# Moving preparation units and masked bundles inside the fourteen-bundle round of a sixteen-head cross attention

## The chip, the core and the metric

The kernel runs on one core of a Trainium2 chip. It is one launch that carries out twelve layers one after the other; the metric is the device time of the whole launch in microseconds. Three runs of the kernel before took 3176.26, 3175.15 and 3161.47 us, median 3175.15 us.

The engines that matter here are TensorE (PE, with its weight loads shown apart as PEld), VectorE (DVE), ScalarE (ACT), GpSimd (POOL) and SyncE (SP), which issues the transfers. Each works through its own list of instructions in order and waits for the others on semaphores.

## The reference, cut to what matters

The seventh layer is the only one that the change touches. Batch 32, 64 queries per batch, 1601 keys, width 128, 16 heads of 8 dimensions; the mask is the same for all batches and heads.

```python
def _L2_xattn_ref(query, key, value, mask, W_q, W_k, W_v, W_o):   # NUM_HEADS 16, D_K 8
    Q = _split(query @ W_q.T)        # query: (32, 64, 128), the normalised x
    K = _split(key @ W_k.T)          # key and value: ctx_1024, (32, 1601, 128)
    V = _split(value @ W_v.T)
    scores = jnp.einsum('bhqd,bhkd->bhqk', Q, K) / jnp.sqrt(jnp.float32(D_K))
    scores = jnp.where(mask, -jnp.inf, scores)
    attn_w = jax.nn.softmax(scores, axis=-1)
    attn_w = jnp.nan_to_num(attn_w, nan=0.0)
    out = jnp.einsum('bhqk,bhkd->bhqd', attn_w, V)
    merged = out.transpose(0, 2, 1, 3).reshape(B, Sq, D_MODEL)
    return merged @ W_o.T
...
x = x + _L2_xattn_ref(_layernorm(x, axis=-1), ctx_1024, ctx_1024, mask_1x1xSxS2_bk1, ...)
```

## The kernel before

The layer is the function `many_head_cross_attention`. It is written as four separate lists, one for each of PE, DVE, ACT and POOL, and all of them walk the same loop variable `b`, the **bundle**. A batch has 14 bundles (`ROUND = 14`): seven steps of 256 keys (the last has 65 keys, one chunk), each for two halves of the heads. I call `b % 14` the **place** in the round, 0 to 13. Thirty-two batches give 448 bundles.

In bundle `b` TensorE does, in this order:

1. `less_max` (L2908; L2911 at the short places 12 and 13): it starts two PSUM banks `st` with minus the maximum of each row. The two instructions (gi 0 and 1) each wait on `exped`: the second may start only when ScalarE has finished the first of the two exponentials of bundle `b - 1`, since `st` has three banks.
2. at the three places in `ON_TENSOR` only, `less_out` (L2921): four matmuls that add the mask to the scores before the exponential.
3. `query_by_keys` (L2895): scores for bundle `b + 18` into `mx`, for the row maxima; these are 512 keys wide, except at places 8 and 9, where they are 65 keys wide. It waits on `topped`, that is until VectorE has read the banks.
4. `keys_by_query` (L2882): the scores of bundle `b` on top of `st`.
5. `values` (L2942): the products of bundle `b - 3` with the values, accumulated in `pv`; at place 3 there are none, and place 4 has two of them and a clearing matmul (L2936). At places 1 and 2 they are for the short step and half as many.
6. `prepare`: at most one preparation unit. All of them use the one bank `prep`, and each waits on `prep_read` until the unit before it has been read out.

A unit is `K` (L2963) or `V` (L2959), a quarter of the projected keys or values of a batch to come, read by ScalarE, `M` (L2967), the maxima turned, read by ScalarE, or one of the three closing units of a batch: `E1` (L2971) turns the result `pvs`; VectorE then computes `own` from it in `own_values` (L3056, L3057, L3058, L3061, four instructions linked by waits); `E2` (L2973) multiplies `own` and cannot start before `own_values` is done; VectorE copies that to `yT` (L3088); `E3` (L2976) applies the output weights, and VectorE adds the result to `x` (L3093). Quarter 3 of K and of V is 65 keys wide and short.

In bundle `b` VectorE does, in this order: `masked_max` (L3031, with L3030) for bundle `b + 18`, two instructions of 512 columns or four of 65; at place 9 the eight small operations of `negated_parts` (L3041 to L3050); unless the place is in `ON_TENSOR`, the mask by a minimum with `capT` after the exponential (L3077, two instructions, each after its exponential); at place 2 the copy of `pv` to `pvs` (L3082); and last what belongs to the E unit of this bundle, for which it waits on `prep_done`. ScalarE does the two exponentials (L3112, L3115) and the read-outs of K, V and M (L3125, L3128, L3131).

Where each unit stands is set by two small tables in the code, `PREPARED` (K and V, counted from place 10 of a round) and the tuple in `late` (M, E1, E2, E3, as a bundle number relative to the batch). Nothing is planned at run time.

Of the kernel before, what the change touches and what calls it, by code (L numbers as in the profile page):

```python
# [2721 lines left out]
def many_head_cross_attention(c, name):  # L2722
# [5 lines left out]
    HELD = 7  # L2728
    FIRST, LAST = -LEAD - ROUND, ROUND * (B - 1) + ROUND + 10
    BUNDLES = ROUND * B  # L2730
    PREPARED = {0: ("K", 0), 2: ("V", 0), 3: ("K", 1), 4: ("V", 1), 5: ("K", 2), 6: ("V", 2), 7: ("K", 3), 9: ("V", 3)}
    ON_TENSOR = (4, 7, 9)
    chunk = [min(P, KEYS - P * j) for j in range(KC)]
    part = [min(4, KC - 4 * m) for m in range(4)]
    with Stage(c, name) as s:
# [27 lines left out]
        V = Steps(s.sem("vector_steps"), (1, ["set"] + LN_V + [f"q{i}" for i in range(4)]))  # L2763
# [11 lines left out]
        def early(b):  # L2775

            n, i = divmod(b - FIRST, ROUND)
            if not 0 <= n < B or i not in PREPARED:
                return None
            kind, m = PREPARED[i]  # L2780
            return kind, n, m

        def late(b):

            for kind, at in (("M", -3), ("E1", 18), ("E2", 20), ("E3", 22)):
                n, off = divmod(b - at, ROUND)
                if off == 0 and 0 <= n < B:
                    return kind, n, 0
            return None

        prep_at = {}
        for b in range(FIRST, LAST):
            for unit in (early(b), late(b)):
                if unit:
                    prep_at[unit] = len(prep_at) + 1
# [6 lines left out]

        masked_here = lambda b: b % ROUND in ON_TENSOR

# [54 lines left out]
        def _(pe):  # L2859
# [119 lines left out]
            for b in range(FIRST, LAST):  # L2979
                now, then = of_bundle(b), of_bundle(b + LEAD)  # L2980
                if now:
                    if b % ROUND == 0:
                        pe.wait_ge(prep_read, prep_at["M", now[0], 0])
                    less_max(b, *now)
                    if masked_here(b):
                        less_out(b, *now[1:])
                if then:
                    n = then[0]
                    if (b + LEAD) % ROUND == 0:
                        pe.wait_ge(qb_made, n + 1)  # L2990
                        pe.wait_ge(prep_read, prep_at["K", n, 3])
                    query_by_keys(b + LEAD, *then)
                if now:
                    keys_by_query(b, *now, 0)
                    keys_by_query(b, *now, 1)
                for x in values_at(b):
                    values(x)
                prepare(early(b))
                prepare(late(b))

        @block.vector
        def _(dve):
# [61 lines left out]
            for b in range(FIRST, LAST):  # L3064
                then = of_bundle(b + LEAD)
                if then:
                    masked_max(b + LEAD, *then)
                    if (b + LEAD) % ROUND == ROUND - 1:
                        negated_parts(then[0])
                now = of_bundle(b)  # L3070
                if now and not masked_here(b):
                    step = now[1]
                    for gi in (0, 1):
                        k, j = (P, (2 * step, 2 * step + 2)) if step < 6 else (KREST, (KC - 1, KC))
                        x = pT[b % HELD][0:k, 0:j[1] - j[0], gi, :].rearrange("p c (h q) -> p c h q", q=S)
                        dve.wait_ge(exped, 2 * b + gi + 1)
                        nc.vector.tensor_tensor(x, x, capT[0:k, j[0]:j[1], :].unsqueeze(2).broadcast_to([k, j[1] - j[0], 4, S]), ALU.min)\  # L3077
                            .then_inc(capped, 1)
                n, off = divmod(b - ROUND - 2, ROUND)
                if off == 0 and 0 <= n < B:  # L3080
                    dve.wait_ge(pv_done, ROUND * (n + 1))
                    nc.vector.tensor_copy(pvs[:, :, :], pv[:, 0:256].rearrange("p (e q) -> p e q", e=2)).then_inc(pv_copied, 1)  # L3082
                unit = late(b)
                if unit and unit[0] == "E1":
                    own_values(unit[1])
                elif unit and unit[0] == "E2":
                    dve.wait_ge(prep_done, prep_at[unit])
                    nc.vector.tensor_copy(yT[:, :], prep[:, 0:S]).then_inc(prep_read, 1)  # L3088
                elif unit and unit[0] == "E3":
                    n = unit[1]  # L3090
                    r = slice(S * (n % 2), S * (n % 2) + S)
                    dve.wait_ge(prep_done, prep_at[unit])
                    nc.vector.tensor_tensor(c.x[r, n // 2, :], prep[r, 0:D], c.x[r, n // 2, :], ALU.add).then_inc(prep_read, 1)  # L3093
# [487 lines left out]
def build(nc, a):  # L3581
    with ExitStack() as ctx:
        c = Core(nc, ctx, a)
        c.turned = nc.dram_tensor("context_turned", (B, P, KEYS), F32).ap()
        start(c)
        cross_attention(c, "L0_xattn", "mask_keys", 1)
        spectral_layer(c, "L0_attn")
        capacity_experts(c, "L0_ffn")
        causal_cross_attention(c, "L1_xattn")
        two_step_attention(c, "L1_attn")  # L3590
        routed_experts(c, "L1_ffn")
        many_head_cross_attention(c, "L2_xattn")
        selective_scan_layer(c, "L2_attn")
        chosen_adapters(c, "L2_ffn")
        kept_cross_attention(c, "L3_xattn", "mask_pairs")
        self_attention(c, "L3_attn")
        quantised_ffn(c, "L3_ffn")
        finish(c)
# [119 lines left out]
```

## Time and profile before

| | |
|---|---|
| profiled execution, its time | 3176.26 us |
| its span, first to last instruction | 3174.5 us |
| median of the three runs | 3175.15 us |
| the layer, first K unit to its last bundles | about 1089 to 2308 us |
| busy in the span: PE / DVE / ACT / POOL | 2655.7 / 2031.4 / 1385.5 / 427.0 us |
| in 1600 to 1700 us: PE / DVE / ACT | 99.99 / 90.07 / 51.45 us |
| length of a round in the steady part | 35.5 us |

A matmul's end is modelled and matmuls overlap, so a PE share near 100% does not say that the array does useful work all the time. What tells more is the start of each group: the distance from one `less_max` to the next is the length of a bundle. Two matmuls in the trace stand for one in the program here, since float32 takes two. The timeline merges neighbouring equal instructions into one row with a count.

### The profile page before, as it was taken

How to read it: one execution, taken by the hardware profiler on the slowest of the kernel's cores; microseconds unless marked ns; L12 is line 12 of the kernel's file. 1: busy time of each engine (PE TensorE's matmuls, PEld its weight loads, DVE VectorE, ACT ScalarE, POOL GpSimd, SP SyncE). 2: the span in 40 equal slices, each digit the busy share in tenths (PEclk: the TensorE clock that was granted, in tenths of full speed). 3: DMA queues.
4: the chain of work that ended last, by engine and by line, in shares of the span. 5: the costliest groups of instructions: out<-in, count | busy, mean ns of one | idle time of the engine just before them, and what ended most of it. 6: DMA issues, size and time to landing. Idle time of an engine off the chain costs nothing. (4 is left out here: it accounts for less than half of the span.)

```text
span 3174.5 us, 65839 instructions
## 1 busy us (share of the span) xinstructions
PE 2655.7 (84%) x26678; PEld 1702.4 (54%) x26678; DVE 2031.4 (64%) x6795; ACT 1385.5 (44%) x2527; POOL 427.0 (13%) x299
## 2 busy tenths in 40 slices
PE   7989553796999699999999999999947989988433
PEld 5767442454666445665556556566524555655323
DVE  5554303576111259899989998998557876536776
ACT  3441211464333225555555555555338964335411
POOL 0000101341000000000000000000004950554100
PEclk9989786897999769999999999999768999899766
DMA  7960041000000100001000100010002210990000
GB/s 238 333 206 1 26 133 29 8 3 16 14 14 14 39 22 23 23 23 33 23 23 23 33 23 23 23 33 2 1 8 80 97 54 6 334 352 26 9 0 14
DMA packets 78239, 188.98 MB, mean 60 GB/s; under 512 B 12418, under 2 KB 46149, under 8 KB 77904
## 3 DMA queue, kind: packets, MB, share of 16 engines
q1 hardware_dynamic: 76912, 182.91, 17.5%
q8 instruction: 212, 3.47, 0.5%
q0 software_dynamic: 1024, 1.85, 0.2%
q14 instruction: 91, 0.75, 0.1%
HBM read 154.19 MB, written 30.79 MB: 58 GB/s over the span
## 5 line engine op out<-in xcount | busy, mean ns | idle before, releaser
L3031 DVE CUSTOM_DVE_ANT_0 L_xattn_junk<-L_xattn_ps_mx,L_xattn_shift 128x512 f32<-128x512 f32 (+1 forms) x1024 | 544.9, 570 | 127.3 <-issue 117.2
L3112 ACT ACTIVATE L_xattn_pT<-L_xattn_ps_st 128x512 f32<-128x512 f32 x768 | 416.9, 594 | 412.4 <-PE L_xattn_ps_st L2882 412.4
L2895 PE MATMUL L_xattn_ps_mx<-L_xattn_kT,L_xattn_qb 32*128 32x512 f32 (+1 forms) x2048 | 496.4, 567 | 1.8 <-DVE L_xattn_tops L3031 1.8
L2882 PE MATMUL L_xattn_ps_st<-L_xattn_qb,L_xattn_kT 32*128 32x256 f32 (+1 forms) x3328 | 463.4, 389 | 0.0
L3077 DVE TENSOR_TENSOR L_xattn_pT<-L_xattn_pT,L_xattn_capT 128x512 f32<-128x512 f32 (+1 forms) x704 | 419.3, 637 | 40.5 <-ACT L_xattn_pT L3112 37.8
L2882 PEld LDWEIGHTS L_xattn_ps_st<-L_xattn_qb,L_xattn_kT 32*128 32x128 f32 (+1 forms) x3328 | 304.1, 183 | 20.7 <-issue 1.2
L2942 PE MATMUL L_xattn_ps_pv<-L_xattn_pT,L_xattn_v 128*17 128x128 f32 x6656 | 267.7, 280 | 0.0
L2942 PEld LDWEIGHTS L_xattn_ps_pv<-L_xattn_pT,L_xattn_v 128*17 128x17 f32 x6656 | 148.4, 98 | 167.0 <-issue 81.0
L2908 PE MATMUL L_xattn_ps_st<-L_xattn_less,L_xattn_ones_b 3*128 3x512 bf16 x768 | 180.6, 390 | 1.4 <-ACT L_xattn_pT L3112 1.2
L1882 DVE SCALAR_TENSOR_TENSOR x<-L_ffn_ps_o,L_ffn_weights,x 128x128 f32<-128x128 f32 x128 | 36.1, 345 | 224.4 <-PE L_ffn_ps_o L1795 224.4
L2895 PEld LDWEIGHTS L_xattn_ps_mx<-L_xattn_kT,L_xattn_qb 32*128 32x128 f32 x2048 | 157.8, 188 | 36.0 <-DVE L_xattn_tops L3031 23.5
L2849 POOL TENSOR_TENSOR L_xattn_qb<-ln_sq,L_xattn_four 128x256 f32<-128x256 f32 x32 | 19.6, 615 | 1105.3 <-PE L_xattn_ps_st L2882 1085.9
L1913 ACT ACTIVATE L_ffn_gelu<-L_ffn_ps_h,L_ffn_b1e 128x512 f32<-128x512 f32 x128 | 87.9, 687 | 163.2 <-PE L_ffn_ps_h L1788 159.9
L1795 PEld LDWEIGHTS L_ffn_ps_o<-L_ffn_w,L_ffn_gelu 128*128 128x128 f32 x1024 | 116.7, 192 | 51.4 <-ACT L_ffn_gelu L1913 51.4
L1795 PE MATMUL L_ffn_ps_o<-L_ffn_w,L_ffn_gelu 128*128 128x128 f32 x1024 | 122.8, 278 | 24.9 <-ACT L_ffn_gelu L1913 24.9
L2959 PE MATMUL L_xattn_ps_prep<-L_xattn_wv,L_xattn_ctxT 128*128 128x128 f32 (+1 forms) x832 | 132.2, 300 | 2.3 <-ACT L_xattn_kT L3125 2.3
L2963 PE MATMUL L_xattn_ps_prep<-L_xattn_ctxT,L_xattn_wk 128*128 128x512 f32 (+1 forms) x256 | 130.1, 592 | 3.1 <-ACT L_xattn_v L3128 2.0
L2959 PEld LDWEIGHTS L_xattn_ps_prep<-L_xattn_wv,L_xattn_ctxT 128*128 128x128 f32 (+1 forms) x832 | 105.2, 196 | 40.4 <-issue 33.1
L2908 PEld LDWEIGHTS L_xattn_ps_st<-L_xattn_less,L_xattn_ones_b 3*128 3x128 bf16 x768 | 45.3, 91 | 135.4 <-ACT L_xattn_pT L3112 75.5
L1788 PE MATMUL L_ffn_ps_h<-xnT,L_ffn_w 128*128 128x512 f32 x256 | 117.4, 602 | 0.0
L2230 ACT ACTIVATE L_attn_xs<-L_attn_xiT,L_attn_bt 128x256 f32<-128x256 f32 x256 | 105.2, 493 | 0.0
L3419 POOL TENSOR_SCALAR L_xattn_out_keys<-L_xattn_mask 128x1536 bf16<-128x1536 uint8 x16 | 78.1, 4883 | 182.0 <-DMA L_xattn_mask<-in_mask_pairs 173.7
(611 smaller groups left out, 4974.5 us busy)
## 6 DMA issues: line engine op xcount, KB each, us to landing
L_xattn_ctxT<-context_turned SPq DMA_DIRECT2D x64, 800.5 KB, 5.9
L_xattn_ctx<-in_ctx SPq DMA_DIRECT2D x64, 768.0 KB
context_turned<-L_xattn_ctxT SPq DMA_DIRECT2D x32, 800.5 KB, 9.6
L_attn_cc<-scratch_rows SPq DMA_DIRECT2D x32, 512.0 KB, 3.7
L_ffn_w<-in_L_ffn_w SPq DMA_DIRECT2D x32, 256.0 KB, 3.2
L_xattn_out_keys<-scratch_q SPq DMA_DIRECT2D x32, 200.1 KB, 10.0
L_ffn_w<-in_L_ffn_W SPq DMA_DIRECT2D x16, 256.0 KB, 3.1
L_xattn_mask<-in_mask_pairs SPq DMA_DIRECT2D x32, 100.1 KB, 15.1
```

The lines of the kernel that those rows point to most:

```text
L1788: nc.tensor.matmul(ph[:, k, :], w1[:, u, P * k:P * k + P], c.xnT[:, 512 * i:512 * i + 512], start=True, stop=True).then_inc(PE.did(f"h{i}{ ...
L1795: last = nc.tensor.matmul(po[:, i % 2, P * j:P * j + P], g[:, i % 2, k, P * j:P * j + P], w2[:, u, k, :], start=(k == 0), stop=(k == FC - 1))
L2230: last = nc.scalar.mul(xs[:, k % 2, j, :], xiT[:, t, :], bt[:, t, n:n + 1])
L2882: last = nc.tensor.matmul(st[0:chunk[j], w % 3, 256 * c2:256 * c2 + 256], kT[n % 3][r:r + 32, P * j:P * j + chunk[j]], qb[n % 3][r:r + 32, ...
L2895: last = nc.tensor.matmul(mx[:, w % 3, to:to + width], qb[n % 3][32 * g:32 * g + 32, 2 * (p % 2):2 * (p % 2) + 2, :].rearrange("p h q -> p ...
L2908: nc.tensor.matmul(st[:, w % 3, :], ones_b[r:r + 3, :], less[n % 2][r:r + 3, :, :].rearrange("p c k -> p (c k)"), start=True, stop=False, ...
L2942: last = nc.tensor.matmul(pv[32 * q:32 * q + 17, P * half:P * half + P], v[n % 3][0:chunk[j], j, 4 * half + q, :], pT[b % HELD][0:chunk[j] ...
L2959: last = nc.tensor.matmul(prep[0:chunk[j], to:to + P], ctxT[:, n % 2, P * j:P * j + chunk[j]], wv[:, :], start=True, stop=True)
L2963: last = nc.tensor.matmul(prep[:, 0:width], wk[:, :], ctxT[:, n % 2, 512 * m:512 * m + width], start=True, stop=True)
L3031: last = nc.vector.tensor_tensor_reduce(out=junk[:, w % 3, to:to + width], in0=mx[:, w % 3, to:to + width], in1=shift[:, k0:k0 + width], s ...
L3077: nc.vector.tensor_tensor(x, x, capT[0:k, j[0]:j[1], :].unsqueeze(2).broadcast_to([k, j[1] - j[0], 4, S]), ALU.min)\
L3112: nc.scalar.activation(pT[b % HELD][:, :, gi, :], st[:, w % 3, :].rearrange("p (c k) -> p c k", c=2), ACT.Exp)\
```

## The change

Three lines of tables change; no instruction is added or removed. In terms of places: V quarter 2 moves from place 2 to 3, and K quarter 3 from place 3 to 4, so that place 2 has no unit; E1, E2 and E3 move from places 4, 6 and 8 to 7, 8 and 9; the three bundles that are masked on TensorE move from places 4, 7 and 9 to 2, 6 and 9.

```diff
@@ many_head_cross_attention
-    PREPARED = {0: ("K", 0), 2: ("V", 0), 3: ("K", 1), 4: ("V", 1), 5: ("K", 2), 6: ("V", 2), 7: ("K", 3), 9: ("V", 3)}
-    ON_TENSOR = (4, 7, 9)
+    PREPARED = {0: ("K", 0), 2: ("V", 0), 3: ("K", 1), 4: ("V", 1), 5: ("K", 2), 7: ("V", 2), 8: ("K", 3), 9: ("V", 3)}
+    ON_TENSOR = (2, 6, 9)
@@ def late(b)
-            for kind, at in (("M", -3), ("E1", 18), ("E2", 20), ("E3", 22)):
+            for kind, at in (("M", -3), ("E1", 21), ("E2", 22), ("E3", 23)):
```

TensorE, places 2 to 4 of a round, before (from the `less_max` of place 2 up to the scores of place 4); `ps_st` are the score banks, `ps_mx` those for the maxima, `ps_pv` the value products, `ps_prep` the preparation bank:

```order
L2908 MATMUL L_xattn_ps_st<-L_xattn_less,L_xattn_ones_b 128x512 x2
L2895 MATMUL L_xattn_ps_mx<-L_xattn_kT,L_xattn_qb 128x512 x2
L2882 MATMUL L_xattn_ps_st<-L_xattn_qb,L_xattn_kT 128x256 x4
L2942 MATMUL L_xattn_ps_pv<-L_xattn_pT,L_xattn_v 17x128 x4
L2959 MATMUL L_xattn_ps_prep<-L_xattn_wv,L_xattn_ctxT 128x128 x4
L2908 MATMUL L_xattn_ps_st<-L_xattn_less,L_xattn_ones_b 128x512 x2
L2895 MATMUL L_xattn_ps_mx<-L_xattn_kT,L_xattn_qb 128x512 x2
L2882 MATMUL L_xattn_ps_st<-L_xattn_qb,L_xattn_kT 128x256 x4
L2963 MATMUL L_xattn_ps_prep<-L_xattn_ctxT,L_xattn_wk 128x65
L2908 MATMUL L_xattn_ps_st<-L_xattn_less,L_xattn_ones_b 128x512 x2
L2921 MATMUL L_xattn_ps_st<-L_xattn_four_turns,L_xattn_shift 128x256 x4
```

The same stretch now:

```order
L2908 MATMUL L_xattn_ps_st<-L_xattn_less,L_xattn_ones_b 128x512 x2
L2921 MATMUL L_xattn_ps_st<-L_xattn_four_turns,L_xattn_shift 128x256 x4
L2895 MATMUL L_xattn_ps_mx<-L_xattn_kT,L_xattn_qb 128x512 x2
L2882 MATMUL L_xattn_ps_st<-L_xattn_qb,L_xattn_kT 128x256 x4
L2942 MATMUL L_xattn_ps_pv<-L_xattn_pT,L_xattn_v 17x128 x4
L2908 MATMUL L_xattn_ps_st<-L_xattn_less,L_xattn_ones_b 128x512 x2
L2895 MATMUL L_xattn_ps_mx<-L_xattn_kT,L_xattn_qb 128x512 x2
L2882 MATMUL L_xattn_ps_st<-L_xattn_qb,L_xattn_kT 128x256 x4
L2959 MATMUL L_xattn_ps_prep<-L_xattn_wv,L_xattn_ctxT 128x128 x4
```

At place 2 the mask has come in and the V unit has gone to place 3, so that only the four short value products stand between the scores of place 2 and the `less_max` of place 3.

TensorE, from E1 to E2, before (places 4 to 6):

```order
L2971 MATMUL L_xattn_ps_prep<-ident,L_xattn_pvs 128x128 x2
L2908 MATMUL L_xattn_ps_st<-L_xattn_less,L_xattn_ones_b 128x512 x2
L2895 MATMUL L_xattn_ps_mx<-L_xattn_kT,L_xattn_qb 128x512 x2
L2882 MATMUL L_xattn_ps_st<-L_xattn_qb,L_xattn_kT 128x256 x4
L2942 MATMUL L_xattn_ps_pv<-L_xattn_pT,L_xattn_v 17x128 x8
L2959 MATMUL L_xattn_ps_prep<-L_xattn_wv,L_xattn_ctxT 65x128
L2908 MATMUL L_xattn_ps_st<-L_xattn_less,L_xattn_ones_b 128x512 x2
L2895 MATMUL L_xattn_ps_mx<-L_xattn_kT,L_xattn_qb 128x512 x2
L2882 MATMUL L_xattn_ps_st<-L_xattn_qb,L_xattn_kT 128x256 x4
L2942 MATMUL L_xattn_ps_pv<-L_xattn_pT,L_xattn_v 17x128 x8
L2973 MATMUL L_xattn_ps_prep<-L_xattn_delta,L_xattn_own 128x64
```

and now (places 7 and 8):

```order
L2971 MATMUL L_xattn_ps_prep<-ident,L_xattn_pvs 128x128 x2
L2908 MATMUL L_xattn_ps_st<-L_xattn_less,L_xattn_ones_b 128x512 x2
L2895 MATMUL L_xattn_ps_mx<-L_xattn_kT,L_xattn_qb 128x65 x4
L2882 MATMUL L_xattn_ps_st<-L_xattn_qb,L_xattn_kT 128x256 x4
L2942 MATMUL L_xattn_ps_pv<-L_xattn_pT,L_xattn_v 17x128 x8
L2973 MATMUL L_xattn_ps_prep<-L_xattn_delta,L_xattn_own 128x64
```

Where two bundles and a V unit stood between E1 and E2 there is now a single bundle.

VectorE, the second maximum of the bundle with E1 and what follows it, before (place 4, masked on TensorE, so that no L3077 stands here) and up to the first maximum of the next bundle:

```order
L3031 ISA L_xattn_junk,L_xattn_tops<-L_xattn_ps_mx,L_xattn_shift 128x512
L3031 ISA L_xattn_tops 128x1
L3056 TENSOR_SCALAR L_xattn_rinv<-L_xattn_ps_prep 128x8
L3057 RECIPROCAL L_xattn_vinv<-L_xattn_rinv 128x8
L3058 TENSOR_TENSOR L_xattn_coef<-L_xattn_vinv,L_xattn_own_dims 128x128
L3061 TENSOR_TENSOR L_xattn_own<-L_xattn_ps_prep,L_xattn_coef 128x128
L3030 MEMSET L_xattn_pause 128x1
L3031 ISA L_xattn_junk,L_xattn_tops<-L_xattn_ps_mx,L_xattn_shift 128x512
```

and now (place 7, which is no longer masked on TensorE):

```order
L3031 ISA L_xattn_junk,L_xattn_tops<-L_xattn_ps_mx,L_xattn_shift 128x512
L3031 ISA L_xattn_tops 128x1
L3077 TENSOR_TENSOR L_xattn_pT<-L_xattn_pT,L_xattn_capT 128x2x256 x2
L3056 TENSOR_SCALAR L_xattn_rinv<-L_xattn_ps_prep 128x8
L3057 RECIPROCAL L_xattn_vinv<-L_xattn_rinv 128x8
L3058 TENSOR_TENSOR L_xattn_coef<-L_xattn_vinv,L_xattn_own_dims 128x128
L3061 TENSOR_TENSOR L_xattn_own<-L_xattn_ps_prep,L_xattn_coef 128x128
L3030 MEMSET L_xattn_pause 128x1
L3031 ISA L_xattn_junk,L_xattn_tops<-L_xattn_ps_mx,L_xattn_shift 128x65
```

The two L3077 now stand ahead of `own_values`.

## Rows read from the trace of the kernel before

**Rows 1.** The page's first part: busy us, share of the span, instructions.
```profile
span 3174.5 us, 65839 instructions
PE 2655.7 (84%) x26678; PEld 1702.4 (54%) x26678; DVE 2031.4 (64%) x6795; ACT 1385.5 (44%) x2527; POOL 427.0 (13%) x299
```
**Rows 2.** Busy by stretch: length, PE, PEld, DVE, ACT, POOL, PE clock, DMA.
```profile
1600.00:1700.00 100.00, 99.99 (x1320) 60.14 (x1319) 90.07 (x378) 51.45 (x104) 1.85 (x3) 1.00 0.08 27
```
**Rows 3.** Waits, 1165 to 2300 us: us in total, times, longest us.
```profile
PEld L_xattn_ps_st L2908 <- ACT L_xattn_pT L3112: 75.5, 193, 1.2
...
DVE L_xattn_rinv L3056 <- PE L_xattn_ps_prep L2971: 10.0, 30, 5.0
...
PEld L_xattn_ps_prep L2973 <- issue: 6.7, 31, 0.4
```
**Rows 4.** Timeline of PE, places 4 to 8: start, us, instruction.
```profile
1601.54 0.27 PE L2936 MATMUL L_xattn_ps_pv<-L_xattn_less,L_xattn_zero_b 32*128 32x256 bf16 x1
...
1603.11 0.70 PE L2895 MATMUL L_xattn_ps_mx<-L_xattn_kT,L_xattn_qb 32*128 32x512 f32 x2
...
1604.29 0.63 PE L2942 MATMUL L_xattn_ps_pv<-L_xattn_pT,L_xattn_v 128*17 128x128 f32 x16
...
1605.22 0.39 PE L2908 MATMUL L_xattn_ps_st<-L_xattn_less,L_xattn_ones_b 3*128 3x512 bf16 x2
...
1606.96 0.43 PE L2973 MATMUL L_xattn_ps_prep<-L_xattn_delta,L_xattn_own 128*128 128x64 f32 x2
1607.33 0.39 PE L2908 MATMUL L_xattn_ps_st<-L_xattn_less,L_xattn_ones_b 3*128 3x512 bf16 x2
...
1609.26 0.63 PE L2942 MATMUL L_xattn_ps_pv<-L_xattn_pT,L_xattn_v 128*17 128x128 f32 x16
1609.83 0.67 PE L2908 MATMUL L_xattn_ps_st<-L_xattn_less,L_xattn_ones_b 3*128 3x512 bf16 x2
1610.12 0.33 PE L2895 MATMUL L_xattn_ps_mx<-L_xattn_kT,L_xattn_qb 32*128 32x65 f32 x2
```
**Rows 5.** Timeline of PE, place 10, then places 2 to 4.
```profile
1614.73 0.57 PE L2908 MATMUL L_xattn_ps_st<-L_xattn_less,L_xattn_ones_b 3*128 3x512 bf16 x2
1615.02 0.70 PE L2895 MATMUL L_xattn_ps_mx<-L_xattn_kT,L_xattn_qb 32*128 32x512 f32 x2
...
1616.10 0.63 PE L2942 MATMUL L_xattn_ps_pv<-L_xattn_pT,L_xattn_v 128*17 128x128 f32 x16
...
1631.84 0.41 PE L2942 MATMUL L_xattn_ps_pv<-L_xattn_pT,L_xattn_v 65*17 65x128 f32 x8
1632.18 1.16 PE L2959 MATMUL L_xattn_ps_prep<-L_xattn_wv,L_xattn_ctxT 128*128 128x128 f32 x8
...
1634.82 0.77 PE L2908 MATMUL L_xattn_ps_st<-L_xattn_less,L_xattn_ones_b 3*128 3x512 bf16 x2
...
1637.05 0.27 PE L2936 MATMUL L_xattn_ps_pv<-L_xattn_less,L_xattn_zero_b 32*128 32x256 bf16 x1
```
**Rows 6.** Timeline of PEld, weight loads that waited (idle before, releaser).
```profile
1610.11 0.09 PEld L2908 LDWEIGHTS L_xattn_ps_st<-L_xattn_less,L_xattn_ones_b 3*128 3x128 bf16 x1 [0.20 <-ACT L_xattn_pT L3112]
...
1635.21 0.09 PEld L2908 LDWEIGHTS L_xattn_ps_st<-L_xattn_less,L_xattn_ones_b 3*128 3x128 bf16 x1 [0.30 <-ACT L_xattn_pT L3112]
```
**Rows 7.** Timeline of DVE: the end of place 4, place 5.
```profile
1603.21 0.17 DVE L3056 TENSOR_SCALAR L_xattn_rinv<-L_xattn_ps_prep 128x8 f32<-128x8 f32 x1 [0.17 <-PE L_xattn_ps_prep L2971]
...
1604.28 0.69 DVE L3031 CUSTOM_DVE_ANT_0 L_xattn_junk<-L_xattn_ps_mx,L_xattn_shift 128x512 f32<-128x512 f32 x1
...
1605.51 1.29 DVE L3077 TENSOR_TENSOR L_xattn_pT<-L_xattn_pT,L_xattn_capT 128x512 f32<-128x512 f32 x2
1606.72 0.69 DVE L3031 CUSTOM_DVE_ANT_0 L_xattn_junk<-L_xattn_ps_mx,L_xattn_shift 128x512 f32<-128x512 f32 x1
```
**Rows 8.** Timeline of ACT: the two exponentials of place 7.
```profile
1609.46 1.09 ACT L3112 ACTIVATE L_xattn_pT<-L_xattn_ps_st 128x512 f32<-128x512 f32 x2 [1.88 <-PE L_xattn_ps_st L2882]
```
**Rows 9.** The clearing matmul, once a batch: count, duration ns, first and last start.
```profile
L2936 PE MATMUL L_xattn_ps_pv<-L_xattn_less,L_xattn_zero_b x32: 267/268/416, 1176.3 to 2269.3; 32*128 32x256 bf16 x32
```

## The prediction

> **What bounds the kernel now.** I read the page's first part, then the busy shares of a stretch inside the layer, its waits, and last the timeline of one round, engine by engine. The change touches one layer, from about 1089 to 2308 us of a span of 3174.5 us [rows 1], so everything is decided there. In a stretch of 100 us of it PE is busy 99.99, DVE 90.07 and ACT 51.45 us, with PE's granted clock at 1.00, which is its level of 2.4 GHz [rows 2]. So TensorE sets the pace, and VectorE, with a tenth of its time free, is close behind: it can be late at one point of a round and idle at another. The layer is periodic: the clearing matmul L2936 starts at 1601.54 [rows 4] and again at 1637.05 [rows 5], so a round takes 35.51 us.
>
> The work of the round is the same before and after: same instructions, same number of masked bundles, same units. Only waits of PE can change the time, so I list them. A wait of the weight loads is not always lost time; the starts of the groups tell. The total that stands out is `less_max` waiting for exponentials, 75.5 us in 193 waits [rows 3], but most of these are about 0.2 us and shorter than the matmuls still in the array.
>
> **The rule behind the present waits.** At place 7, which has no unit, the value products start at 1609.26 and the first `less_max` of place 8 at 1609.83 [rows 4]; its second one has to wait until 1610.11 for the exponential [rows 6]. The exponentials of place 7 start at 1609.46 and take 1.09 us for the two, the second starting half a microsecond after the first [rows 8], so the first ends near 1610.05 and PE goes on 0.06 us later. So the second `less_max` cannot start earlier than 0.85 us after the value products of the bundle before it. What stands between (products 0.57, a unit at least 0.37) is the cover. With products and a unit there is 0.94 and no loss: from 1605.22 to 1607.33 the bundle of place 6 takes 2.11 us [rows 4]. Without a unit 0.28 us is missing. In today's round three bundles lack cover:
> - place 8, behind place 7 without a unit: 1609.83 to 1610.12, 0.29 us [rows 4];
> - place 10, behind place 9 without a unit: from 1614.73 to its maxima at 1615.02 [rows 5]. The products follow at 1616.10, 1.37 us after the first `less_max`, where at place 5 they follow 1.18 us after (1603.11 to 1604.29) [rows 4]. So a wait in a bundle with full maxima costs 0.19 us and 0.10 us is got back. I count 0.19.
> - place 4, behind place 3, which has a short unit and no products: 1634.82 [rows 5] to 1635.21 [rows 6], 0.39 us.
>
> Sum 0.87 us per round, the most that a better placing of units could win.
>
> **The change part by part.**
>
> *The units V2 and K3 moved, the mask at place 2.* Place 3 now carries the long V unit behind its scores, place 4 has the double products, so the wait of 0.39 us at place 4 goes. Place 2 has lost its unit and keeps only short products, 0.34 us (1631.84 to 1632.18) [rows 5]. Place 3 thus waits 0.85 − 0.34 = 0.51 us, of which 0.10 comes back: cost 0.41. Change about +0.02 us, nothing.
>
> *The mask at 6 instead of 7, E units behind places 7, 8 and 9.* Place 6 has no unit now; place 7 waits 0.28 and pays 0.18. The waits at 8 and 10 go, as places 7 and 9 have an E unit: −0.29 − 0.19. Together −0.30 us.
>
> So the cover alone gives −0.28 us per round (0.87 to 0.59). The masked bundles cost PE the same wherever they stand, and VectorE is spared three bundles as before.
>
> *E1, E2, E3 in neighbouring bundles.* This adds the wait that I expect to decide. E2 multiplies `own`, which VectorE computes from E1. Today E1 ends place 4, masked on TensorE, so VectorE has no minimum to do and begins `own_values` at 1603.21, as soon as E1 is through; it is done when the next maximum starts at 1604.28 [rows 7], 1.07 us later. E2 comes at 1606.96 [rows 4] and never waits: its load shows only the ordinary 6.7 us of issue in 31 times [rows 3], 0.2 each. In the new order E1 ends place 7, where VectorE has maxima and both minima ahead of `own_values`. Take m for the start of the maxima matmuls of place 7.
> - VectorE: its first maximum starts at m + 1.17 (1603.11 to 1604.28); two maxima take 1.23 (to 1605.51); two minima 1.21 (to 1606.72) [rows 4, 7]; `own_values` 1.07. Done at m + 4.68, and E2 may start at about m + 4.74 with the signal of 0.06. The exponentials don't hold the minima back: they start about when the products do [rows 4, 8], at m + 1.3, and the second ends by m + 2.4.
> - TensorE: products at m + 1.08 (1615.02 to 1616.10) [rows 5], 0.57 for them, 0.37 for E1 (as E2 from 1606.96 to 1607.33), so place 8 starts at m + 2.02; E2 would come 1.74 us into it (1605.22 to 1606.96) [rows 4], at m + 3.76.
>
> PE waits 4.74 − 3.76 = 0.98 us at E2. Queued behind it on PE are the `less_max`, mask and scores of place 9, so ScalarE and all later bundles slip too. VectorE is not late afterwards: it goes on with the four short maxima and the minima of place 8 and copies `yT` near m + 6.8; E3 is due near m + 7.6. Its final add follows `negated_parts` and ends near m + 9.3, while the next unit, K0, wants the bank near m + 9.7. Both these waits I cost at nothing, with 0.8 and 0.4 us of cover; these times are estimates, made by laying the bundles of rows 4 and 7 end to end.
>
> Bounds of this term: below, if VectorE ran `own_values` straight behind E1 as today, nothing; above, if a lag of VectorE from place 5 (2.44 us of maxima and minima against a bundle of 2.11 us) reached place 7, 0.33 us more, so 1.3. I take 0.98, since place 6 is masked on TensorE: its maxima come some 0.8 us later and VectorE has no minima there, so the lag is gone.
>
> The Trainium skill, "TensorE: Matmul & The Clock Gate", in the step-by-step part on loading weights, says that PE's window may pull weight loads ahead of matmuls in flight when row groups don't conflict, while matmuls keep their order. If that reached past a waiting instruction, the loads of place 9 would be done under the wait at E2 and some of it would come back. In this trace it does not: the maxima matmuls of place 8 use other rows than the waiting `less_max` and still start only at 1610.12, behind it [rows 4, 6].
>
> **The sum.** −0.28 + 0.98 = +0.70 us per round. The clearing matmul runs 32 times, from 1176.3 to 2269.3 us [rows 9]; in the first round no batch has come to its E units, and in the last three the K and V units and then the maxima have ended, so 28 rounds have all parts. 28 × 0.70 = 19.6, and about 1 us for the others, where VectorE or the exponentials set the pace and E2 waits in part: +20.6. The profiled execution took 3176.26 us (span 3174.5), which gives 3196.9. That execution is 1.1 us above the median of the three runs, 3175.15, so against the median I forecast **3196 us**, 0.65% longer.
>
> **The rivals.**
> - *A. The wait at E2 stays away* (not slower). If VectorE were through with the minima of place 7 before PE reaches E2, the change would only cover exponentials: 28 × −0.28 = −8 us, 3167. It decides at own_values ending before m + 3.76. For it: VectorE has 10% free. Against it: the free time lies elsewhere in the round, and program order puts both minima ahead.
> - *B. The lag spreads.* E3 waits for `yT`, or K0 for the final add, behind `negated_parts` at place 9. K0 has just 0.4 us of cover; if VectorE runs 0.5 us later than I reckon at E2 and so 0.1 to 0.5 at K0 too, a round costs 0.5 to 0.7 more: 3196 + 28 × 0.6 = 3213. Against it: after the wait at E2 PE is late by the same amount as VectorE.
> - *C. All cover waits vanish, and E2 too.* If the even spacing of masks at 2, 6, 9 kept both engines so far apart that no `less_max` waits, 28 to 31 × −0.87: about −26 us, 3149. Against it: place 3 has less cover than any bundle now.
> - *D. The clock falls* in the longer pause. Today PE runs at clock 1.00 through pauses of 0.4 us [rows 2, 6]. Were it at the lower level of 1.2 GHz for 1 us of each round, 28 × 0.5 = 14 us more: 3210. The Trainium skill, "TensorE: Matmul & The Clock Gate", in its part on what matters for kernels, warns of idle gaps between bursts; no run here shows a pause near 1 us in this layer.
>
> **How the numbers follow.** My forecast 0.68, A 0.14, B 0.10, C 0.04, D 0.04. Own range of the forecast: E2's wait 0.8 to 1.2 gives 3191 to 3202, and runs differ by some 0.2%, so 3186 to 3206. The range for 8 in 10 takes in most of A and the lower part of B and D: 3168 to 3209. A measurement of this kernel can hardly tell less than 0.5% (16 us) from no change, that is 3159 to 3191. Slower by over 0.5%: of the forecast 0.53, B 0.10, D 0.04, together 0.67. Within: 0.15 of the forecast and 0.10 of A, 0.25. Faster: C 0.04 and, with a low run as the one of 3161.47, 0.04 of A, 0.08.
>
> **What would show it.** In the profile of the changed kernel: a round of about 36.2 us; at place 8 a load of L2973 idle for 0.9 to 1.3 us with L3061 as its releaser, about 30 times (none today); the 10.0 us that L3056 waits for E1 [rows 3] gone; the wait at L2908 of place 3 near 0.5 us and those of places 4, 8 and 10 gone; PE's clock still at 1.00. I am wrong if L2973 does not wait, or if a round is 35.5 us or less; and in a step if K0 (L2963) or E3 (L2976) wait for VectorE, or if place 3 does not wait.

## The result and the profile after

The changed kernel takes 3256.85 us (median of four runs, 3253.93 to 3260.91) against 3175.68 us for the kernel before on the same chip: ratio 1.0268, 95% interval 1.0236 to 1.0299. The direction was forecast, the size was not: 3196 us, with a range up to 3209. The profiled execution took 3256.58 us, its span 3254.8.

The page's first part, in the columns of [rows 1]:

```profile
span 3254.8 us, 65809 instructions
PE 2704.6 (83%) x26648; PEld 1727.7 (53%) x26678; DVE 2027.0 (62%) x6795; ACT 1387.9 (43%) x2527; POOL 426.4 (13%) x299
```

VectorE and ScalarE do what they did. TensorE is busy 49 us longer though the program has the same instructions [rows 1] (30 matmul records are missing from the trace), so they take longer, and the span grows by 80.3.

Three rows of the waits, 1165 to 2380 us (us in total, times, longest), answer to [rows 3]:

```profile
PEld L_xattn_ps_st L2908 <- ACT L_xattn_pT L3112: 76.1, 192, 1.2
...
PEld L_xattn_ps_prep L2973 <- DVE L_xattn_own L3061: 31.6, 30, 1.1
...
PE L_xattn_ps_prep L2973 <- DVE L_xattn_own L3061: 23.2, 30, 0.8
```

The forecast wait is there, 30 times, with L3061 as releaser. PE is idle for 23.2 us in all before it. That is of the size of the forecast 20 us, and not 80.

The rest is in the spacing of the rounds. The timeline of PE, the clearing matmul alone, five in a row (in the columns of [rows 4]):

```profile
1624.12 0.27 PE L2936 MATMUL L_xattn_ps_pv<-L_xattn_less,L_xattn_zero_b 32*128 32x256 bf16 x1
...
1663.51 0.27 PE L2936 MATMUL L_xattn_ps_pv<-L_xattn_less,L_xattn_zero_b 32*128 32x256 bf16 x1
...
1699.80 0.27 PE L2936 MATMUL L_xattn_ps_pv<-L_xattn_less,L_xattn_zero_b 32*128 32x256 bf16 x1
...
1739.18 0.27 PE L2936 MATMUL L_xattn_ps_pv<-L_xattn_less,L_xattn_zero_b 32*128 32x256 bf16 x1
...
1777.02 0.27 PE L2936 MATMUL L_xattn_ps_pv<-L_xattn_less,L_xattn_zero_b 32*128 32x256 bf16 x1
```

These rounds take 39.39, 36.29, 39.38 and 37.84 us. One work list has three lengths. Of the 28 steady rounds 8 take 36.3 us, 8 take 37.8 and 12 take 39.4. The forecast was 36.2. The timeline of PE around E2, in the first of them (39.39):

```profile
1630.58 0.70 PE L2895 MATMUL L_xattn_ps_mx<-L_xattn_kT,L_xattn_qb 32*128 32x512 f32 x2
...
1633.88 0.63 PE L2942 MATMUL L_xattn_ps_pv<-L_xattn_pT,L_xattn_v 128*17 128x128 f32 x16
...
1635.29 0.44 PE L2973 MATMUL L_xattn_ps_prep<-L_xattn_delta,L_xattn_own 128*128 128x64 f32 x2 [0.78 <-DVE L_xattn_own L3061]
1635.65 0.39 PE L2908 MATMUL L_xattn_ps_st<-L_xattn_less,L_xattn_ones_b 3*128 3x512 bf16 x2
...
1638.51 1.05 PE L2942 MATMUL L_xattn_ps_pv<-L_xattn_pT,L_xattn_v 128*17 128x128 f32 x16
1639.49 0.69 PE L2976 MATMUL L_xattn_ps_prep<-L_xattn_wo,L_xattn_yT 128*64 128x128 f32 x2
1640.12 0.61 PE L2908 MATMUL L_xattn_ps_st<-L_xattn_less,L_xattn_ones_b 3*128 3x512 bf16 x2
...
1642.36 1.06 PE L2942 MATMUL L_xattn_ps_pv<-L_xattn_pT,L_xattn_v 128*17 128x128 f32 x16
```

and in the second (36.29):

```profile
1674.68 0.43 PE L2973 MATMUL L_xattn_ps_prep<-L_xattn_delta,L_xattn_own 128*128 128x64 f32 x2 [0.78 <-DVE L_xattn_own L3061]
1675.05 0.39 PE L2908 MATMUL L_xattn_ps_st<-L_xattn_less,L_xattn_ones_b 3*128 3x512 bf16 x2
...
1676.99 0.63 PE L2942 MATMUL L_xattn_ps_pv<-L_xattn_pT,L_xattn_v 128*17 128x128 f32 x16
1677.56 0.43 PE L2976 MATMUL L_xattn_ps_prep<-L_xattn_wo,L_xattn_yT 128*64 128x128 f32 x2
1677.92 0.39 PE L2908 MATMUL L_xattn_ps_st<-L_xattn_less,L_xattn_ones_b 3*128 3x512 bf16 x2
```

The same pause of 0.78 us stands in both (0.84 us by the starts: PE could have gone on 0.57 us after the products began, at 1634.45, and went on at 1635.29). In the first, sixteen value products behind it take 1.05 us instead of 0.63, and E3's pair of matmuls 0.69 instead of 0.43. The next bundle is long too. The granted clock says why. Busy by stretch, in the columns of [rows 2]:

```profile
1634.00:1638.00 4.00, 3.22 (x40) 2.18 (x34) 3.48 (x28) 1.07 (x2) 0.00 (x0) 0.83 0.00 0
1638.00:1641.00 3.00, 3.00 (x30) 1.58 (x30) 1.77 (x14) 1.09 (x2) 0.00 (x0) 0.50 0.00 0
1641.00:1644.00 3.00, 3.00 (x30) 1.45 (x22) 1.73 (x7) 1.09 (x2) 0.00 (x0) 0.59 0.00 0
1644.00:1648.00 4.00, 4.00 (x60) 2.01 (x58) 3.25 (x10) 2.35 (x5) 0.00 (x0) 1.00 0.00 0
...
1674.00:1678.00 4.00, 3.32 (x46) 2.05 (x48) 3.79 (x33) 1.36 (x3) 0.00 (x0) 1.00 0.00 0
...
1180.00:2230.00 1050.00, 1025.70 (x12671) 609.35 (x12670) 880.14 (x3677) 515.70 (x1022) 17.15 (x28) 0.95 0.07 23
...
2310.00:2350.00 40.00, 38.83 (x347) 21.63 (x339) 19.88 (x78) 14.04 (x28) 0.00 (x0) 0.62 0.01 1
2350.00:2390.00 40.00, 37.25 (x313) 20.41 (x306) 12.44 (x29) 9.53 (x20) 0.00 (x0) 0.50 0.00 1
```

From 1638 to past 1641 PE runs at 0.50, its level of 1.2 GHz, and is back at 2.4 GHz by 1644. With the shares of the neighbouring rows the low level lasts from about 1636.6 to 1643.5, some 6.8 us (an estimate from these rows). In the round of 36.29 the same bundles run at 1.00. Over the steady 1050 us the clock is 0.95 in the mean. The kernel before has 1.00 there:

```profile
1180.00:2230.00 1050.00, 1049.92 (x13604) 628.12 (x13597) 948.72 (x3947) 548.33 (x1093) 17.83 (x29) 1.00 0.07 24
```

The row of the clearing matmul, answering to [rows 9], closes the sum:

```profile
L2936 PE MATMUL L_xattn_ps_pv<-L_xattn_less,L_xattn_zero_b x32: 267/268/417, 1171.5 to 2349.3; 32*128 32x256 bf16 x32
```

First to last is 1177.8 us, where it was 1093.0 [rows 9]: +84.8. Of it, 28 × 0.79 = 22.1 us is the undisturbed round, 36.29 for 35.50 (the sums of the median bundle lengths). 8 × 1.55 + 12 × 3.1 = 49.6 is the low clock in steady rounds. The three other rounds take 112.08 for 98.89 us, 13.2 more. Together that is 84.9. Near the end of the layer little work is left, and the clock is low in the kernel before too. There the last clearing matmul, at 2269.3 us, ends a stretch at 0.91; in the changed kernel it comes at 2349.3 us, at the end of one at 0.62, so the fall comes about one batch earlier. The kernel before:

```profile
2230.00:2270.00 40.00, 38.69 (x466) 23.02 (x464) 30.72 (x112) 18.57 (x36) 0.00 (x0) 0.91 0.01 2
2270.00:2310.00 40.00, 37.25 (x313) 20.40 (x302) 11.17 (x27) 9.50 (x20) 0.00 (x0) 0.50 0.00 1
```

The first clearing matmul comes 4.8 us sooner, as the time before it differs from execution to execution (it starts between 1161.8 and 1177.5 us in the traces of this case). That leaves +80, the span's difference. So some 20 us are waits, and some 60 are clock.

### The profile page after: what moved, and what is told of

Same layout as the page of the kernel before. It is cut to its first block and busy times, and to the rows that moved or that the text cites. A ratio compares the mean times of both kernels' runs of the same rounds, so it can differ in the third digit from the quotient of the medians.

```text
span 3254.8 us, 65809 instructions
## 1 busy us (share of the span) xinstructions
PE 2704.6 (83%) x26648; PEld 1727.7 (53%) x26678; DVE 2027.0 (62%) x6795; ACT 1387.9 (43%) x2527; POOL 426.4 (13%) x299
## 5 line engine op out<-in xcount | busy, mean ns | idle before, releaser
L2895 PE MATMUL L_xattn_ps_mx<-L_xattn_kT,L_xattn_qb 32*128 32x512 f32 (+1 forms) x2048 | 518.3, 593 | 2.2 <-DVE L_xattn_tops L3031 2.2
L2882 PE MATMUL L_xattn_ps_st<-L_xattn_qb,L_xattn_kT 32*128 32x256 f32 (+1 forms) x3328 | 499.6, 412 | 0.0
L3077 DVE TENSOR_TENSOR L_xattn_pT<-L_xattn_pT,L_xattn_capT 128x512 f32<-128x512 f32 (+1 forms) x704 | 419.1, 636 | 33.5 <-ACT L_xattn_pT L3112 28.6
L2882 PEld LDWEIGHTS L_xattn_ps_st<-L_xattn_qb,L_xattn_kT 32*128 32x128 f32 (+1 forms) x3328 | 328.6, 195 | 22.7 <-issue 1.2
L2942 PE MATMUL L_xattn_ps_pv<-L_xattn_pT,L_xattn_v 128*17 128x128 f32 x6656 | 283.2, 292 | 0.0
L3125 ACT COPY L_xattn_kT<-L_xattn_ps_prep 128x512 f32<-128x512 f32 (+1 forms) x128 | 63.1, 493 | 103.2 <-PE L_xattn_ps_prep L2963 103.2
```

What stands on the lines that cost most here:

```text
L2882: last = nc.tensor.matmul(st[0:chunk[j], w % 3, 256 * c2:256 * c2 + 256], kT[n % 3][r:r + 32, P * j:P * j + chunk[j]], qb[n % 3][r:r + 32, ...
L2895: last = nc.tensor.matmul(mx[:, w % 3, to:to + width], qb[n % 3][32 * g:32 * g + 32, 2 * (p % 2):2 * (p % 2) + 2, :].rearrange("p h q -> p ...
L2942: last = nc.tensor.matmul(pv[32 * q:32 * q + 17, P * half:P * half + P], v[n % 3][0:chunk[j], j, 4 * half + q, :], pT[b % HELD][0:chunk[j] ...
```

## The experiments

Each kernel was timed beside the kernel before on the same chip. The ratios are against that, with 95% intervals. Theory 1 of the expectations is that the wait at E2 is what brings the clock down; later ones ask what else is needed. The code cuts leave out lines, marked by `...`. "Steady clock" is the granted clock from 1180 to 2230 us; a "slow round" is one of the 28 steady rounds that is 1.5 us or more over the kernel's own shortest, counted in the one profiled execution.

**Is it the wait?** `own_first` puts `own_values` ahead of both minima of place 7.

```diff
+                unit = late(b)
+                if unit and unit[0] == "E1":
+                    own_values(unit[1])
                 if now and not masked_here(b):
...
-                unit = late(b)
-                if unit and unit[0] == "E1":
-                    own_values(unit[1])
-                elif unit and unit[0] == "E2":
+                if unit and unit[0] == "E2":
```

> The changed kernel with one thing turned round on VectorE: at place 7 own_values comes ahead of the two minima (L3077) instead of behind them. Theory 1 (the pause of about 0.84 us in which PE waits for own at E2 costs itself and makes the clock fall): no wait at L2973, round 36.29 - 0.84 = 35.45 us, clock 1.00 in the layer, time 3174 us, equal to the kernel before within 0.5%. Rival 2 (the clock falls because units and masked bundles now stand in the row 6, 7, 8, 9, whatever the pause): rounds of 37 to 38.5 us, clock about 0.95, time near 3230 us.

Measured: 3177.94 us, 1.0010 [0.9995, 1.0025]. No wait at L2973 in the steady part, rounds of 35.45 and 35.69, steady clock 1.00:

```profile
1180.00:2230.00 1050.00, 1044.53 (x13536) 626.64 (x13534) 936.12 (x3930) 550.56 (x1091) 17.83 (x29) 1.00 0.07 23
```

With the three table lines in place and only two items of VectorE exchanged, the whole loss of 80 us is gone. The wait at E2 is necessary for both parts of it.

`own_mid` puts it between the two minima:

```diff
                     for gi in (0, 1):
+                        if gi == 1 and own_due:
+                            own_values(unit[1])
...
```

> The changed kernel with own_values between the two minima of place 7. The wait at E2 shrinks from 0.84 us to about 0.25 us. Theory 1: if a short pause leaves the clock alone, round 35.7 us, clock 1.00, time 3182 us; if any added wait at this point were enough for a fall, rounds above 37 us still come and the time is over 3220 us. Rival 2: about 3240 us.

Measured: 3181.68 us, 1.0020 [1.0001, 1.0039]. PE waits 0.2 us a round, a round takes 35.69, steady clock 1.00. A pause of 0.2 us costs its length.

`pause_half` adds one minimum of 256 columns there, into a tile `idle` that nothing reads, so that PE waits 0.5 us (edit against `own_mid`):

```diff
...
                         if gi == 1 and own_due:
+                            nc.vector.tensor_tensor(idle[:, :], cap[:, 0:256], cap[:, 0:256], ALU.min)
                             own_values(unit[1])
...
```

> As own_mid, with one more minimum operation of 256 columns on VectorE (into a tile that nothing reads) ahead of own_values at place 7: the wait at E2 is about 0.6 us, between the 0.84 us of the changed kernel and the 0.25 us of own_mid. Theory 1 (thin stretch and pause together, the longer the pause the more rounds are hit): full-clock rounds of 36.0 us; some are hit, fewer than the 20 of 28 of the changed kernel: 3200 to 3230 us. If the fall needs nearly the whole 0.84 us: none hit, 3191 us.

Measured: 3218.94 us, 1.0123 [1.0093, 1.0153]. 9 of 28 rounds are slow (six of 39.1 us, three of 37.6, the others 36.02 to 36.25), steady clock 0.98. The waits of PE in `own_mid`, then in `pause_half`, 1165 to 2400 us (the line numbers shift with the edit):

```profile
PE L_xattn_ps_prep L2973 <- DVE L_xattn_own L3061: 6.3, 30, 1.1
...
PE L_xattn_ps_prep L2974 <- DVE L_xattn_own L3062: 16.4, 31, 1.1
```

In this place, with 0.2, 0.5 and 0.8 us of pause, 0, 9 and 20 rounds are slow: the clock's share grows with the pause and has no value of its own per pause.

**Is it that TensorE is idle, or the length of the round?** The next kernels put matmuls with zero weights (they add nothing to `pv`) where the pause was. `filled` has nine with 32 rows:

```diff
                 prepare(early(b))
+                if now and late(b) and late(b)[0] == "E2":
+                    for _ in range(9):
+                        nc.tensor.matmul(pv[:, 0:256], zero_b[0:32, :], less[now[0] % 2][0:32, 0, :], start=False, stop=False)
                 prepare(late(b))
```

> The changed kernel with nine extra matmuls (zero weights, 256 columns in bf16, added to the value bank, so that they add nothing) on PE just ahead of E2 at place 8: about 0.97 us of array work in place of the 0.84 us pause, everything else as in the changed kernel. Theory 1: the clock stays at 1.00 and every round takes about 36.4 us, time 3200 us: the pause's own length remains, the fall goes. Rival 2: rounds of 36.3, 37.8 and 39.4 us as in the changed kernel, 3257 us.

Measured: 3249.24 us, 1.0224 [1.0190, 1.0257]. PE no longer waits at E2, yet 11 of 28 rounds are slow (nine of 39.6 us and two of 38.1, the others 36.52) and the steady clock is 0.97. The expectation missed: work in a quarter of the rows only lessens the effect, though PE is busy nearly all the time:

```profile
1180.00:2230.00 1050.00, 1046.56 (x13108) 629.18 (x13105) 892.48 (x3722) 523.51 (x1037) 17.22 (x28) 0.97 0.07 23
```

`filled_full` uses all 128 rows:

```diff
-                        nc.tensor.matmul(pv[:, 0:256], zero_b[0:32, :], less[now[0] % 2][0:32, 0, :], start=False, stop=False)
+                        nc.tensor.matmul(pv[:, 0:256], zero_b[:, :], less[now[0] % 2][:, 0, :], start=False, stop=False)
```

> As filled, but the nine extra matmuls ahead of E2 use all 128 rows of the array instead of 32, again with zero weights. If it is the time without a running matmul that matters, as many rounds are hit as in filled (about 10 of 28) and the time is near 3245 us. If the used part of the array counts, fewer or none are hit: every round 36.5 us, 3205 us.

Measured: 3195.33 us, 1.0064 [1.0046, 1.0082]. All steady rounds take 36.33 us, steady clock 1.00. Its timeline of PE at place 8 and its stretch:

```profile
1642.95 1.16 PE L3001 MATMUL L_xattn_ps_pv<-L_xattn_less,L_xattn_zero_b 128*128 128x256 bf16 x9
1643.94 0.33 PE L2973 MATMUL L_xattn_ps_prep<-L_xattn_delta,L_xattn_own 128*128 128x64 f32 x2
```
```profile
1180.00:2230.00 1050.00, 1046.45 (x13536) 636.81 (x13528) 920.65 (x3847) 539.43 (x1069) 17.82 (x29) 1.00 0.07 23
```

E2 starts 0.99 us after the fillers, so the round has lost as much as to the pause. But the kernel is 61 us faster than the changed one, by work that has no use. What is left over the kernel before, 20.0 us, is within a microsecond of the forecast 20.6: the sum for the waits was right, in part by luck (see below), and all the rest is the clock. The two fillers also show that the busy time of the profile is not what counts: the 32-row matmuls left PE as busy (1046.56 us of 1050) as the full ones.

`filled_at_6` puts the same nine full matmuls ahead, at place 6, and keeps the pause (edit against `filled_full`):

```diff
-                if now and late(b) and late(b)[0] == "E2":
+                if now and b % ROUND == 6:
```

> The changed kernel with its pause at E2 left as it is; the nine extra matmuls (128 rows, zero weights, about 1 us) stand at the end of place 6 instead, which had no unit. They also cover the 0.28 us wait of place 7, so a round at full clock takes about 36.3 + 0.7 = 37.0 us. Theory 1 (the whole stretch of places 6 to 9 counts): fewer or no rounds are hit, clock near 1.00, 3217 to 3235 us. Rival (the pause alone, at this distance from the dense part): rounds are hit as in the changed kernel, up to 40 us, over 3265 us.

Measured: 3289.77 us, 1.0362 [1.0342, 1.0382]. The shortest round is 37.1 us; 22 of 28 are slow, steady clock 0.94. `filled_at_9` has them behind it (`b % ROUND == 9`, before E3):

> The changed kernel with its pause left as it is and the nine extra matmuls (128 rows, zero weights, 1 us) at place 9, ahead of E3, the other side of the pause from filled_at_6. Full-clock rounds of 37.3 us. Theory N: more work beside the pause, in the bundle of the short maxima, keeps the clock up: few or no rounds hit, 3230 us. Rival (only the length of the pause counts at this place): hit as before, over 3275 us.

Measured: 3268.50 us, 1.0310 [1.0272, 1.0347]; shortest round 37.38, 15 of 28 slow, steady clock 0.96. In both, few or no slow rounds were expected under theory 1 and theory N; that missed. Dense work two bundles ahead of the pause doesn't buy it off; one bundle behind it, it helps a little (15 slow rounds for 20).

**Which lines of the change?** `masks_only` is the kernel before with the new mask places:

```diff
-    ON_TENSOR = (4, 7, 9)
+    ON_TENSOR = (2, 6, 9)
```

> The kernel before with only the masked places changed, to 2, 6 and 9; all units where they were. E1 at place 4 is now behind two minima on VectorE, so V3 at place 5 waits about 0.34 us; the waits at places 4, 8 and 10 stay. Theory 1: round 35.7 us, clock 1.00, 3182 us. Rival 2 (the masks' places make the clock fall): falls, over 3200 us.

Measured: 3191.86 us, 1.0064 [1.0048, 1.0079]; round 36.22 where I expected 35.7. Here too `own_values` got behind two minima, at place 4, and now the V unit of place 5 has to wait until `own_values` has read the bank. Timeline of PE, waits (columns as above) and stretch:

```profile
1610.69 0.43 PE L2959 MATMUL L_xattn_ps_prep<-L_xattn_wv,L_xattn_ctxT 128*65 128x128 f32 x2 [0.85 <-DVE L_xattn_own L3061]
```
```profile
PEld L_xattn_ps_prep L2959 <- DVE L_xattn_own L3061: 32.8, 29, 1.1
...
PE L_xattn_ps_prep L2959 <- DVE L_xattn_own L3061: 24.7, 29, 0.9
```
```profile
1180.00:2230.00 1050.00, 1025.24 (x13313) 615.00 (x13309) 920.48 (x3856) 542.15 (x1073) 17.82 (x29) 1.00 0.07 23
```

This pause is as long as the one at E2, and PE is busy 1025 of 1050 us, as in the changed kernel. But the clock stays at 1.00. So neither length nor busy share decides alone, nor is it a masked bundle behind the pause, which both have. What differs is where it stands: the bundles around place 5 have maxima of 512 columns, while the pause at E2 stands between places 8 and 9, whose maxima are 65 wide.

`e_only` is the kernel before with the E units at 7, 8, 9 and the masks left at 4, 7, 9:

```diff
-            for kind, at in (("M", -3), ("E1", 18), ("E2", 20), ("E3", 22)):
+            for kind, at in (("M", -3), ("E1", 21), ("E2", 22), ("E3", 23)):
```

> The kernel before with only E1, E2 and E3 moved, to places 7, 8 and 9; the masks stay at 4, 7 and 9, so E1's bundle has no minima. Theory 1: no wait at L2973, the waits at places 4 and 7 remain (0.39 and 0.28), those of 8 and 10 go; round 35.2 us, clock 1.00, 3168 us. Rival 2 (E units in neighbouring bundles make the clock fall): over 3220 us.

Measured: 3171.34 us, 0.9986 [0.9969, 1.0003]; round 35.22, no wait at L2973, clock 1.00. `mask_279` is the changed kernel with the mask of place 6 at 7:

```diff
-    ON_TENSOR = (2, 6, 9)
+    ON_TENSOR = (2, 7, 9)
```

> The changed kernel with the masked bundles at places 2, 7 and 9 instead of 2, 6 and 9, so that the bundle with E1 has no minima on VectorE. Theory 1: no wait at L2973, round about 35.4 us, clock 1.00, 3174 us. Rival 2 (units and masks in the row 7, 8, 9): clock still falls, over 3220 us.

Measured: 3170.76 us, 0.9983 [0.9969, 0.9996]; round 35.34, clock 1.00. The bundle with E1 is masked on TensorE, VectorE has no minima ahead of `own_values`, and nothing waits. The neighbouring E units alone cost nothing, the masks alone 0.6%, and the whole change, with V2 and K3 moved too, 2.7%.

**The pause away from the short maxima.** `pause_5` is the kernel before with two more minima ahead of `own_values` (into a tile `idle` that nothing reads), so that the V unit of place 5 waits:

```diff
                 if unit and unit[0] == "E1":
+                    nc.vector.tensor_tensor(idle[:, 0, :], cap[:, 0:512], cap[:, 0:512], ALU.min)
+                    nc.vector.tensor_tensor(idle[:, 1, 0:448], cap[:, 0:448], cap[:, 0:448], ALU.min)
                     own_values(unit[1])
```

> The kernel before with two extra minimum operations on VectorE (960 columns, about 1.1 us, into a tile that nothing reads) ahead of own_values at place 4. The V unit of place 5 then waits about 0.6 us for the bank and the maxima of place 6 about 0.3 us more. Theory 1a (a pause of PE of this size makes the clock fall wherever it stands in the round): rounds of 36.4 us with some of 38 and 39.5, clock under 1.00, time over 3230 us. Theory 1b (the pause does it only together with the thin work of places 7 to 9, E units, short maxima, a masked bundle): every round about 36.4 us, clock 1.00, 3200 us.

Measured: 3196.77 us, 1.0079 [1.0063, 1.0094]; round 36.13, steady clock 1.00. It is weaker than meant: PE waits 0.28 us at the V unit, and of the loss of 0.63 us a round place 5 has 0.35 and places 6 and 8 0.14 and 0.13, where VectorE is late with the maxima. So it doesn't test a pause of 0.8 us. `pause_full_maxima` keeps the changed kernel's pause at E2 and moves E1 and E2 to places 5 and 6, with nothing masked on TensorE there (E3 goes to place 8, V3 to 7 and one mask from 6 to 7):

```diff
-    PREPARED = {0: ("K", 0), 2: ("V", 0), 3: ("K", 1), 4: ("V", 1), 5: ("K", 2), 7: ("V", 2), 8: ("K", 3), 9: ("V", 3)}
-    ON_TENSOR = (2, 6, 9)
+    PREPARED = {0: ("K", 0), 2: ("V", 0), 3: ("K", 1), 4: ("V", 1), 5: ("K", 2), 7: ("V", 2), 8: ("K", 3), 11: ("V", 3)}
+    ON_TENSOR = (2, 7, 9)
-            for kind, at in (("M", -3), ("E1", 21), ("E2", 22), ("E3", 23)):
+            for kind, at in (("M", -3), ("E1", 19), ("E2", 20), ("E3", 22)):
```

> The changed kernel with the same chain of units two places earlier: E1 at place 5, E2 at 6, E3 at 8, V3 at 7, masks at 2, 7 and 9. E1's bundle has its minima on VectorE as before, so E2 waits about 0.9 us, but now between bundles whose maxima are 512 columns wide. Theory N (the clock falls only when the pause lies beside the short maxima of places 8 and 9, where half of the array has little to do): no round is hit, clock 1.00, round 36.1 us, 3195 us. Rival E (it is the E units themselves around the pause): rounds are hit as in the changed kernel, over 3235 us.

Measured: 3194.79 us, 1.0060 [1.0042, 1.0078]; every steady round 36.19 us. Timeline and stretch:

```profile
1614.38 0.43 PE L2973 MATMUL L_xattn_ps_prep<-L_xattn_delta,L_xattn_own 128*128 128x64 f32 x2 [0.78 <-DVE L_xattn_own L3061]
```
```profile
1180.00:2230.00 1050.00, 1023.85 (x13327) 614.65 (x13326) 925.08 (x3858) 542.60 (x1075) 17.78 (x29) 1.00 0.07 24
```

The same 0.78 us, at the same instruction, behind the same VectorE work, cost only their length among full maxima. This is the pair to carry: a pause of 0.8 us brought the clock down in the thin stretch of the round, and in neither of the two other places tried. That it is the short maxima which make the stretch thin enough is inferred from these places and from the fillers; no run widens them with the pause left in, and E3, one mask and V3 moved in this kernel as well.

**A version that beats both.** `respread` leaves the masks at 2, 6, 9, puts E1 at place 6, masked on TensorE, with a bundle between it and E2, and spreads the units so that fewer neighbours lack one:

```diff
-    PREPARED = {0: ("K", 0), 2: ("V", 0), 3: ("K", 1), 4: ("V", 1), 5: ("K", 2), 6: ("V", 2), 7: ("K", 3), 9: ("V", 3)}
-    ON_TENSOR = (4, 7, 9)
+    PREPARED = {0: ("K", 0), 2: ("V", 0), 4: ("K", 1), 5: ("V", 1), 6: ("K", 2), 7: ("V", 2), 9: ("K", 3), 11: ("V", 3)}
+    ON_TENSOR = (2, 6, 9)
-            for kind, at in (("M", -3), ("E1", 18), ("E2", 20), ("E3", 22)):
+            for kind, at in (("M", -3), ("E1", 20), ("E2", 22), ("E3", 23)):
```

> All units placed by the two findings: every bundle that needs cover has a unit (long V2 at place 3, K3 at 5, V3 at 7), the two places without a unit are 4 (double products) and 13 (short exponentials), the masks are at 2, 6 and 9, E1 is at the masked place 6, E2 at 8 and E3 at 9. No wait of less_max over 0.1 us, none at L2973: round 34.65 us, clock 1.00, 28 x -0.85 = -24 us and a little more at the ends: 3149 us, ratio 0.992. If the waits that I take away are refilled by VectorE's lag (the rival here), the round stays at 35.2 to 35.5 us.

Measured: 3151.97 us, 0.9927 [0.9909, 0.9946], 0.7% faster than the kernel before. The round is 34.83 us (0.18 over the expectation, mostly at place 0), steady clock 1.00:

```profile
1180.00:2230.00 1050.00, 1049.11 (x13847) 635.86 (x13840) 954.34 (x4018) 557.00 (x1109) 17.82 (x29) 1.00 0.07 24
```

## Why the prediction was wrong

*What bounds the kernel* held: TensorE sets the pace, and only its waits changed. The rule of 0.85 us of cover, worked out from the rows of place 7, held too: places 3 and 7 wait, and 4, 8 and 10 no longer.

*"0.10 us is got back"* was wrong. Place 3 takes 2.78 us and pays 0.50, place 7 takes 2.40 and pays 0.29, both in full, where I charged 0.41 and 0.18. Together they are 0.20 a round too low. I had read the return from place 10 alone.

*The wait at E2* was rightly placed and its mechanism right, but smaller: 0.84 us instead of 0.98. PE was ready at m + 3.87 (forecast 3.76) and started at m + 4.71 (4.74), m being 1630.58 in the round shown. Place 7's products started 1.18 us behind its maxima and not 1.08: it is the same 0.10 us that does not come back, so one misreading made the covers too cheap and this wait too long, and by luck the two nearly cancel: +0.79 for +0.70 a round, a round of 36.29 for "about 36.2". E3 and K0 wait for nothing, so rival B did not come; rivals A and C fail by the wait itself.

*The step that failed* is the price of a pause. I charged it with its length and wrote that the clock would still be at 1.00. In fact PE fell to 1.2 GHz in 20 of 28 steady rounds, which cost 49.6 us, and a batch earlier at the layer's end, most of the 13.2 us there. That is rival D: its mechanism was the right one, but I gave it a chance of 0.04 and a size of 0.5 us a round, when it measured 1.8, so that even its 3210 was 47 us short. The 0.5 assumed one microsecond at the low level. A fall lasts longer, some 6.8 us in the stretch above, and everything on PE in it goes slow. In the steady part of the changed kernel the low stretches have two lengths, some 3.4 and some 6.8 us, and they cost the 1.55 and the 3.1 us by which the rounds differ.

The evidence that I gave for the small chance was that PE runs at 1.00 through pauses of 0.4 us. The rows don't show such pauses: those waits are of weight loads, while PE itself is busy 99.99 of 100 us [rows 2] and 1049.92 of 1050, and its list of waits in the steady part is empty. So the kernel before could say nothing of how the clock takes a pause, and above all not of the place. The prediction names the four short maxima beside E2, and uses them only for VectorE's time; that TensorE has thin work there was not weighed. The Trainium skill, "TensorE: Matmul & The Clock Gate", in the part on a second failure mode, speaks of a kernel whose TensorE idles briefly but often between groups and whose clock then swings between its two levels. The changed kernel agrees with that in kind, at pauses of 0.78 us once a round; `masks_only` and `pause_full_maxima` show that such pauses need not do it.

Shown by experiments: the wait at E2 is needed for the loss (`own_first`), about 20 us of it are the waits and 61 the clock (`filled_full`), and a pause as long among full maxima leaves the clock alone (`pause_full_maxima`, `masks_only`). Not settled: how much work, at which distance, is enough. `filled_at_9` with dense work behind the pause still has 15 slow rounds, `filled` 11, and no rule that I can state gives these counts. Rounds with equal work differ by when the fall comes: in the changed kernel, between 1180 and 2230 us, the twelve low stretches that begin 0.65 to 2.09 us after E2 starts last 6.8 us, the seven that begin 2.11 to 2.69 us after it last 3.4. What sets that moment is open.

## What to carry to other kernels

Before charging a new pause on TensorE with its length, look at what it does on both sides of it: where the work next to the pause is thin (here bundles with maxima of 65 instead of 512 columns), price the granted clock as well, by the work that would run at half of it. If a kernel's rounds have several distinct lengths with one work list, look at the clock of short stretches before any wait. A chain through another engine (E1, `own_values`, E2) has to be placed with the order of that engine in view: two neighbouring bundles did for it when VectorE had no minima ahead of `own_values` in the first, and not otherwise.

## What the runs showed that I had not expected

- Useless work can make a kernel faster: nine full matmuls in place of a pause, 3256.85 to 3195.33 us.
- The rows count: nine with 32 rows instead of 128 left PE equally busy and the kernel at 3249.24 us.
- The fall comes after the pause, not in it: the pause ends at 1635.29, the clock falls at about 1636.6, and E3 is still slow at 1639.49. At its level of 1.2 GHz sixteen value products take 1.05 us instead of 0.63.
- Effects of tables don't add: nothing and 0.6% alone were 2.7% together. The masks alone put `own_values` late and a pause among full maxima; with the E units moved as well, the same pause stands beside the short ones.
